# Local attention: new step orders for four engines, and new places for the first steps of the next stage

## What is computed

```python
def attn_layer(x, Wqkv, qs, ksc, Wo):            # 16 heads of 64, window 32
    q, k, v = split(x @ Wqkv)                    # 128 -> 3 x 1024
    q = l2norm(q) * qs;  k = l2norm(k) * ksc     # then a rotary embedding on both
    out = local_attention(q, k, v)               # each window sees itself and the window before it
    return out @ Wo                              # 1024 -> 128
def ffn_layer(x, g, bln, W1, b1, W2, b2):
    xn = layernorm(x) * g + bln
    a, gate = split(xn @ W1 + b1)                # 128 -> 2 x 341
    return a * gelu(gate) @ W2 + b2
for i in range(6):
    x = attn_layer(shift_tokens(x), ...) + x
    x = ffn_layer(shift_tokens(x), ...) + x
```

## Time and profile before

| what | us |
|---|---|
| median of 3 runs (lowest, highest) | 1986.94 (1985.29, 1989.4) |
| the profiled execution | 1985.58 |
| span of the profiled execution | 1983.8 |
| PE matmul busy in the span | 1823.7 |
| windowed_layers | about 109.6 to 1746 of the span |

### The profile page before, as it was taken

The page is one execution under the profiler, slowest core; times in us unless marked ns, Lnnn a source line. Parts: engine busy times, 40 slices in busy tenths (PEclk is TensorE's granted clock), DMA queues, the critical chain, the costliest instruction groups (busy, mean ns, idle before and its releaser), DMA issues. The chain is left out here.

```text
span 1983.8 us, 78949 instructions
## 1 busy us (share of the span) xinstructions
PE 1823.7 (92%) x32837; PEld 1278.3 (64%) x32837; DVE 1430.1 (72%) x2605; ACT 1138.5 (57%) x2379; POOL 1435.6 (72%) x1838
## 2 busy tenths in 40 slices
PE   4769999999999999999999999999999999788948
PEld 3636666666666666666666666666666676566638
DVE  2268778778777788787878787877788778455546
ACT  1136666666566566666666566656666666335425
POOL 1168888879788888888888788978898888222334
PEclk9789999999999999999999999999999999889969
DMA  3022131111311113111113111121111101030012
GB/s 101 1 41 56 44 99 52 47 45 51 101 48 48 51 48 100 49 50 48 48 48 103 48 48 46 34 85 32 32 35 36 42 24 35 10 98 1 23 35 71
DMA packets 60837, 99.93 MB, mean 50 GB/s; under 512 B 15848, under 2 KB 35065, under 8 KB 58643
## 3 DMA queue, kind: packets, MB, share of 16 engines
q1 hardware_dynamic: 58978, 91.72, 16.0%
q0 software_dynamic: 1504, 3.17, 0.5%
HBM read 44.50 MB, written 21.45 MB: 33 GB/s over the span
## 5 line engine op out<-in xcount | busy, mean ns | idle before, releaser
L1273 PE MATMUL b_bank_proj<-layer_weights,b_stream_t 128*128 128x512 f32 x1152 | 591.6, 615 | 13.6 <-DVE b_plain_moved L1069 9.7
L1069 DVE TENSOR_TENSOR b_plain_moved<-b_bank_proj,b_rope 128x1024 f32<-128x1024 f32 x384 | 467.6, 1221 | 100.2 <-ACT b_squares L903 96.9
L812 POOL TENSOR_TENSOR b_rotated<-b_plain_moved 128x1024 f32<-128x1024 f32 x192 | 453.4, 2361 | 45.4 <-DVE b_plain_moved L1069 45.4
L827 POOL TENSOR_TENSOR b_rotated<-b_rotated,b_inv_norm 128x1024 f32<-128x1024 f32 x192 | 365.3, 1902 | 15.1
L903 ACT ACTIVATE b_squares<-b_bank_proj 128x512 f32<-128x512 f32 x384 | 229.2, 597 | 248.4 <-PE b_bank_proj L1273 243.4
L1273 PEld LDWEIGHTS b_bank_proj<-layer_weights,b_stream_t 128*128 128x128 f32 x1152 | 187.9, 191 | 117.1 <-issue 57.1
L1075 DVE TENSOR_REDUCE b_norm<-b_squares 128x16 f32<-128x1024 f32 x192 | 232.2, 1209 | 42.7 <-ACT b_squares L903 42.4
L1281 PEld LDWEIGHTS b_bank_shared<-const_tables,b_rotated 128*128 128x128 f32 x1536 | 180.6, 143 | 72.2 <-issue 67.4
L1281 PE MATMUL b_bank_shared<-const_tables,b_rotated 128*128 128x128 f32 x1536 | 211.9, 276 | 3.8 <-POOL b_rotated L827 1.7
L832 POOL TENSOR_TENSOR b_probs<-b_probs,b_inv_sum 128x512 f32<-128x512 f32 x192 | 200.3, 1047 | 14.0 <-DVE b_inv_sum L1090 13.8
L1347 PEld LDWEIGHTS b_bank_shared<-b_attended_t,layer_weights 128*128 128x128 f32 x1536 | 182.9, 192 | 25.6 <-issue 23.9
(11 more groups left out here) (346 smaller groups left out, 2889.7 us busy)
## 6 DMA issues: line engine op xcount, KB each, us to landing
b_v_shifted<-b_v SPq DMA_DIRECT2D x192, 192.0 KB, 2.5
sorted_rows<-sorted_rows SPq DMA_DIRECT2D x66, 258.0 KB, 3.2
layer_weights<-L_ffn_Wqkv SPq DMA_DIRECT2D x6, 1536.0 KB
b_v_shifted<-b_v SPq DMA_DIRECT2D x72, 128.0 KB
layer_weights<-L_ffn_Wo SPq DMA_DIRECT2D x6, 512.0 KB
c_sorted_in<-sorted_rows SPq DMA_DIRECT2D x23, 129.0 KB, 2.0
layer_weights<-L_ffn_w SPq DMA_DIRECT2D x8, 256.0 KB, 5.9
c_w<-L_ffn_w SPq DMA_DIRECT2D x8, 256.0 KB, 5.7
```

Source lines behind the costliest of these rows:

```text
L812: nc.gpsimd.tensor_tensor(out=turned[:, k, :], in0=pm[:, k, 0, :], in1=pm[:, k, 1, :], op=ALU.add).then_inc(add_done, 1)
L827: nc.gpsimd.tensor_tensor(out=tk, in0=tk, in1=repeat_last(rn[:, k, :], DH), op=ALU.mult).then_inc(rope_done, 1)
L1069: nc.vector.tensor_tensor(to, src.to_broadcast(shape), tab.to_broadcast(shape), ALU.mult).then_inc(mul_done, 1)
L1273: nc.tensor.matmul(out, xs[:, b, t * P:(t + 1) * P], w, start=True, stop=True).then_inc(proj_full, 1)
```

## The change

All four tables are written anew, each with the steps that it had (a step may stand at another place of the turn, with another `ahead`), and the steps of the next stage hang behind other steps. No instruction is added, removed or altered; SP's list stays. The shared PSUM banks follow the new order.

```diff
--- before.py
+++ after.py
@@ -488,57 +488,58 @@
 
 
 PE_TURN = [
-    ("heads_t", 0, 0), ("heads_t", 0, 1), ("project", 0, 5), ("probs_t", -2, 1), ("project", 1, 0), ("project", 1, 1),
-    ("down", -2, 0), ("project", 1, 2), ("pv", -2, 0), ("project", 1, 3), ("heads_t", 0, 2), ("heads_t", 0, 3),
-    ("probs_t", -1, 0), ("project", 1, 4), ("scores", 0, 0), ("project", 1, 5), ("heads_t", 1, 0), ("project", 2, 0),
-    ("project", 2, 1), ("heads_t", 1, 1), ("probs_t", -1, 1), ("out", -2, 0), ("project", 2, 2), ("enter", 1, 0),
-    ("pv", -1, 0), ("project", 2, 3), ("heads_t", 1, 2), ("heads_t", 1, 3), ("out", -1, 0), ("scores", 1, 0),
-    ("back", -1, 0), ("project", 2, 4), ("project", 2, 5), ("probs_t", 0, 0), ("probs_t", 0, 1), ("heads_t", 2, 0),
-    ("project", 3, 0), ("heads_t", 2, 1), ("project", 3, 1), ("pv", 0, 0), ("project", 3, 2), ("norm_t", -1, 0),
-    ("project", 3, 3), ("out", 0, 0), ("heads_t", 2, 2), ("heads_t", 2, 3), ("up", -1, 0), ("scores", 2, 0),
-    ("up", -1, 1), ("up", -1, 2), ("up", -1, 3), ("probs_t", 1, 0), ("project", 3, 4), ("project", 3, 5),
-    ("probs_t", 1, 1), ("project", 4, 0), ("project", 4, 1), ("pv", 1, 0), ("heads_t", 3, 0), ("heads_t", 3, 1),
-    ("project", 4, 2), ("out", 1, 0), ("heads_t", 3, 2), ("heads_t", 3, 3), ("up", -1, 4), ("up", -1, 5),
-    ("leave", -2, 0), ("scores", 3, 0), ("project", 4, 3), ("project", 4, 4), ("probs_t", 2, 0),
+    ("scores", -1, 0), ("probs_t", -2, 1), ("project", 0, 5), ("project", 1, 0), ("leave", -3, 0), ("heads_t", 0, 0),
+    ("project", 1, 1), ("heads_t", 0, 1), ("down", -2, 0), ("pv", -2, 0), ("project", 1, 2), ("project", 1, 3),
+    ("heads_t", 0, 2), ("heads_t", 0, 3), ("probs_t", -1, 0), ("project", 1, 4), ("scores", 0, 0), ("heads_t", 1, 0),
+    ("project", 1, 5), ("project", 2, 0), ("probs_t", -1, 1), ("project", 2, 1), ("heads_t", 1, 1), ("out", -2, 0),
+    ("project", 2, 2), ("pv", -1, 0), ("project", 2, 3), ("heads_t", 1, 2), ("heads_t", 1, 3), ("out", -1, 0),
+    ("project", 2, 4), ("back", -1, 0), ("scores", 1, 0), ("enter", 2, 0), ("project", 2, 5), ("project", 3, 0),
+    ("probs_t", 0, 0), ("probs_t", 0, 1), ("project", 3, 1), ("heads_t", 2, 0), ("pv", 0, 0), ("project", 3, 2),
+    ("norm_t", -1, 0), ("heads_t", 2, 1), ("project", 3, 3), ("heads_t", 2, 2), ("heads_t", 2, 3), ("probs_t", 1, 0),
+    ("up", -1, 0), ("up", -1, 1), ("scores", 2, 0), ("up", -1, 2), ("up", -1, 3), ("heads_t", 3, 0),
+    ("project", 3, 4), ("project", 3, 5), ("probs_t", 1, 1), ("project", 4, 0), ("project", 4, 1), ("pv", 1, 0),
+    ("project", 4, 2), ("out", 0, 0), ("heads_t", 3, 1), ("up", -1, 4), ("up", -1, 5), ("heads_t", 3, 2),
+    ("out", 1, 0), ("project", 4, 3), ("heads_t", 3, 3), ("probs_t", 2, 0), ("project", 4, 4),
 ]
 
 
 ACT_TURN = [
-    ("heads_t", 0, 1), ("probs_t", -2, 1), ("project", 1, 2), ("root", 1, 0), ("exp", -1, 1), ("attended", -2, 0),
-    ("project", 1, 3), ("heads_t", 0, 2), ("heads_t", 0, 3), ("project", 1, 4), ("attended", -2, 1),
-    ("probs_t", -1, 0), ("project", 1, 5), ("root", 1, 1), ("project", 2, 0), ("exp", 0, 0), ("project", 2, 1),
-    ("heads_t", 1, 0), ("heads_t", 1, 1), ("probs_t", -1, 1), ("exp", 0, 1), ("root", 2, 0), ("project", 2, 2),
-    ("attended", -1, 0), ("attended", -1, 1), ("enter", 1, 0), ("project", 2, 3), ("heads_t", 1, 2),
-    ("heads_t", 1, 3), ("back", -1, 0), ("project", 2, 4), ("project", 2, 5), ("probs_t", 0, 0), ("exp", 1, 0),
-    ("probs_t", 0, 1), ("project", 3, 0), ("project", 3, 1), ("heads_t", 2, 0), ("root", 2, 1), ("heads_t", 2, 1),
-    ("attended", 0, 0), ("attended", 0, 1), ("project", 3, 2), ("project", 3, 3), ("exp", 1, 1), ("root", 3, 0),
-    ("heads_t", 2, 2), ("heads_t", 2, 3), ("gelu", -1, 0), ("gelu", -1, 1), ("gelu", -1, 2), ("probs_t", 1, 0),
-    ("project", 3, 4), ("project", 3, 5), ("probs_t", 1, 1), ("root", 3, 1), ("project", 4, 0), ("project", 4, 1),
-    ("exp", 2, 0), ("exp", 2, 1), ("attended", 1, 0), ("attended", 1, 1), ("root", 4, 0), ("project", 4, 2),
-    ("heads_t", 3, 0), ("heads_t", 3, 1), ("heads_t", 3, 2), ("heads_t", 3, 3), ("project", 4, 3), ("project", 4, 4),
-    ("exp", 3, 0), ("leave", -2, 0), ("heads_t", 4, 0), ("probs_t", 2, 0), ("project", 4, 5), ("project", 5, 0),
-    ("root", 4, 1), ("project", 5, 1),
+    ("root", -1, 1), ("heads_t", -1, 0), ("exp", -2, 0), ("project", 0, 2), ("root", 0, 0), ("exp", -2, 1),
+    ("attended", -3, 0), ("attended", -3, 1), ("heads_t", -1, 1), ("heads_t", -1, 2), ("project", 0, 3),
+    ("heads_t", -1, 3), ("project", 0, 4), ("probs_t", -2, 0), ("root", 0, 1), ("project", 0, 5), ("exp", -1, 0),
+    ("leave", -3, 0), ("project", 1, 0), ("probs_t", -2, 1), ("project", 1, 1), ("heads_t", 0, 0), ("heads_t", 0, 1),
+    ("root", 1, 0), ("exp", -1, 1), ("attended", -2, 0), ("project", 1, 2), ("project", 1, 3), ("heads_t", 0, 2),
+    ("heads_t", 0, 3), ("project", 1, 4), ("attended", -2, 1), ("root", 1, 1), ("probs_t", -1, 0), ("project", 1, 5),
+    ("project", 2, 0), ("exp", 0, 0), ("exp", 0, 1), ("project", 2, 1), ("probs_t", -1, 1), ("heads_t", 1, 0),
+    ("heads_t", 1, 1), ("project", 2, 2), ("attended", -1, 0), ("attended", -1, 1), ("root", 2, 0), ("project", 2, 3),
+    ("heads_t", 1, 2), ("heads_t", 1, 3), ("back", -1, 0), ("project", 2, 4), ("project", 2, 5), ("enter", 2, 0),
+    ("project", 3, 0), ("probs_t", 0, 0), ("probs_t", 0, 1), ("project", 3, 1), ("root", 2, 1), ("exp", 1, 0),
+    ("exp", 1, 1), ("heads_t", 2, 0), ("attended", 0, 0), ("project", 3, 2), ("attended", 0, 1), ("heads_t", 2, 1),
+    ("project", 3, 3), ("root", 3, 0), ("heads_t", 2, 2), ("heads_t", 2, 3), ("gelu", -1, 0), ("gelu", -1, 1),
+    ("probs_t", 1, 0), ("gelu", -1, 2), ("project", 3, 4), ("project", 3, 5), ("probs_t", 1, 1), ("project", 4, 0),
+    ("project", 4, 1),
 ]
 
 
 DVE_TURN = [
-    ("share", 1, 0), ("mul", 3, 2), ("scale", -1, 0), ("mul", 3, 3), ("share", 1, 1), ("norms", 3, 1),
-    ("residual", 0, 0), ("hidden", -1, 0), ("soft", 2, 0), ("soft", 2, 1), ("norms", 4, 0), ("mul", 4, 0),
-    ("share", 2, 0), ("mul", 4, 1), ("mul", 4, 2), ("share", 2, 1), ("residual", 1, 0), ("hidden", -1, 1),
-    ("hidden", -1, 2), ("soft", 3, 0), ("mul", 4, 3), ("norms", 4, 1), ("share", 3, 0), ("soft", 3, 1), ("mul", 5, 0),
-    ("norms", 5, 0), ("mul", 5, 1), ("down", -1, 0), ("mul", 5, 2), ("share", 3, 1), ("mul", 5, 3), ("norms", 5, 1),
-    ("soft", 4, 0), ("soft", 4, 1), ("mul", 6, 0), ("norms", 6, 0), ("mul", 6, 1), ("share", 4, 0),
-    ("residual", 2, 0), ("mul", 6, 2), ("share", 4, 1), ("mul", 6, 3), ("norms", 6, 1), ("residual", 3, 0),
-    ("soft", 5, 0), ("stats", 0, 0), ("soft", 5, 1), ("mul", 7, 0), ("mul", 7, 1), ("norms", 7, 0),
+    ("share", 2, 0), ("hidden", -1, 1), ("hidden", -1, 2), ("share", 2, 1), ("residual", 0, 0), ("residual", 1, 0),
+    ("mul", 4, 3), ("norms", 4, 1), ("soft", 3, 0), ("soft", 3, 1), ("share", 3, 0), ("mul", 5, 0), ("norms", 5, 0),
+    ("mul", 5, 1), ("down", -1, 0), ("share", 3, 1), ("mul", 5, 2), ("norms", 5, 1), ("mul", 5, 3), ("soft", 4, 0),
+    ("soft", 4, 1), ("mul", 6, 0), ("share", 4, 0), ("mul", 6, 1), ("norms", 6, 0), ("share", 4, 1),
+    ("residual", 2, 0), ("mul", 6, 2), ("mul", 6, 3), ("residual", 3, 0), ("norms", 6, 1), ("stats", 0, 0),
+    ("soft", 5, 0), ("soft", 5, 1), ("mul", 7, 0), ("mul", 7, 1), ("norms", 7, 0), ("share", 5, 0), ("scale", 0, 0),
+    ("mul", 7, 2), ("mul", 7, 3), ("norms", 7, 1), ("share", 5, 1), ("soft", 6, 0), ("hidden", 0, 0), ("soft", 6, 1),
+    ("mul", 8, 0), ("norms", 8, 0), ("mul", 8, 1), ("mul", 8, 2),
 ]
 
 
 POOL_TURN = [
-    ("clamp", 5, 0), ("add", 5, 0), ("rope", 5, 0), ("weigh", 3, 1), ("clamp", 5, 1), ("add", 5, 1), ("rope", 5, 1),
-    ("clamp", 6, 0), ("add", 6, 0), ("weigh", 4, 0), ("rope", 6, 0), ("weigh", 4, 1), ("add", 6, 1), ("clamp", 6, 1),
-    ("rstd", 0, 0), ("rope", 6, 1), ("clamp", 7, 0), ("add", 7, 0), ("weigh", 5, 0), ("weigh", 5, 1), ("clamp", 7, 1),
-    ("rope", 7, 0), ("add", 7, 1), ("clamp", 8, 0), ("rope", 7, 1), ("weigh", 6, 0), ("add", 8, 0), ("rope", 8, 0),
-    ("weigh", 6, 1), ("add", 8, 1), ("clamp", 8, 1), ("weigh", 7, 0), ("rope", 8, 1),
+    ("clamp", 7, 1), ("clamp", 8, 0), ("rope", 7, 1), ("add", 8, 0), ("weigh", 6, 0), ("weigh", 6, 1), ("rope", 8, 0),
+    ("clamp", 8, 1), ("add", 8, 1), ("rope", 8, 1), ("weigh", 7, 0), ("clamp", 9, 0), ("add", 9, 0), ("rope", 9, 0),
+    ("weigh", 7, 1), ("clamp", 9, 1), ("add", 9, 1), ("rope", 9, 1), ("weigh", 8, 0), ("add", 10, 0),
+    ("clamp", 10, 0), ("weigh", 8, 1), ("rope", 10, 0), ("add", 10, 1), ("clamp", 10, 1), ("rstd", 1, 0),
+    ("rope", 10, 1), ("weigh", 9, 0), ("clamp", 11, 0), ("add", 11, 0), ("rope", 11, 0), ("weigh", 9, 1),
+    ("add", 11, 1),
 ]
 
 
@@ -548,14 +549,13 @@
 
 
 FIRST = {
-    "pe": {("back", TURNS - 1, 0): ("f_weights",), ("norm_t", TURNS - 1, 0): ("f_contexts",),
-            ("up", TURNS - 1, 1): ("f_normed", "f_keys",), ("up", TURNS - 1, 3): ("f_queries",),
```

(11 more changed lines are left out.)

## The result

The changed kernel takes 2041.78 us (median of 4 runs, 2033.55 to 2054.86) against 1986.45 (4 runs, 1985.29 to 1989.4) on the same chip: a ratio of 1.028, interval 1.0253 to 1.0307. It is **slower by 55 us**, where 1981 with a range of 1965 to 1996 was forecast. Its runs also lie 21 us apart, those of before 4. The profiled execution took 2039.08 us, span 2037.3, so 53.5 us of span are to be found.

The account below looks back on a forecast made before the run. TensorE was taken to bound the kernel, 97% busy in the middle. -8.2 - 4.6 + 3.4 + 2.4 + 1.1 = -5.9 on the profiled 1985.58 gave 1979.7, as a median 1981.0 us; range 1965 to 1996.

Parts of the forecast that it names:

- Part 2: PE's dense steps: fetch waits follow the count of matmuls between them; pv gains, scores unchanged: -4.6 us, bounds -13.1 to +4.9.
- Part 5: Moves costed at nothing, such as probs_t t0.1 coming 1.30 instead of 2.60 us ahead of pv t0, called covered.
- Part 3: PE, back one projection behind out t3, ahead of scores t1: a wait of 0.14 us, 24 times, +3.4 us.
- Part 1: DVE, mul ahead of norms for the next turn's tile 0: removes 0.34 us of PE waiting a turn, -8.2 us.
- Part 4: POOL's chain behind back: heads t2.2 and probs_t t1.0 wait slightly for POOL, +2.4 us, bounds 0 and +15.8.
- Rival C: Slower: POOL becomes the bound behind back, waits of 0.66 us a turn stand; 1994 to 1997 us; chance 0.21.
- Part 6: Start and end of the stage: norms loses its free place at the start, +1.1 us; the drain 0, bounds -2 and +2.
- The rivals: Fetch waits fall by half, 1965 (0.13); nothing that can be told, 1989 or 1985.6 (0.26); slower through POOL, 1994 to 1997 (0.21).
- what would prove it wrong: L1306's waits growing over 5 us, new PE waits for POOL over 10 us in the middle, or L1335's idle time halving.
- S: The experiments' theory, not the prediction's: a late last semaphore ahead of a dense step delays the request for PE's next instruction block.

Follow-up runs that it names:

- act_probs2: Kernel before, with ACT copying the second half of t2's transposed probabilities ahead of two of its other steps, PE's order unchanged; 1976.85 us, ratio 0.9926.
- before_sc0: Kernel before, with pv of the tile two before ahead of project 1.2 on PE, instead of behind it; 2015.25 us, ratio 1.0125.
- before_back: Kernel before, with back one projection behind out t3, ahead of scores t1, and t3's residual ahead of norms on the DVE; 2006.47 us, ratio 1.0073.
- dve_mul: Kernel before, with mul ahead of norms for the next turn's tile 0 on the DVE; 1989.53 us, ratio 0.999.
- after_pv3: Changed kernel, with the old order around out t2 again on PE and ACT (project, heads, then probs_t); 2025.9 us, ratio 1.0198.
- slack_pv0: Kernel before, with act_probs2's move and the transposed shares of t0 one projection earlier on PE and ACT; 1972.48 us, ratio 0.9937.
- after_all: Changed kernel, with all six local undos together and project 1.2's square moved ahead of root, exp and copy on ACT; 2008.96 us, ratio 1.0122.

## Why the prediction was wrong, point by point

- **Part 2 failed, and with it the forecast.** Its -4.6 for the dense steps measured +39.0. The step that failed is "I count in PE_TURN the matmuls between the last pv, scores or out and each pv": act_probs2 changed the waits of pv t2 from 7.9 to 1.4 us with no matmul moved. That fetch was the cause of "issue" was right; what sets its start was not. The sentence "scores begins with eight wide mask matmuls, behind which the issue can catch up, so I leave its 15.0 as it is" failed too: 33.7. The upper bound of +9.5 for scores came from the same count (its 62 is 64 by the table) and was too low by half.
- **Part 5 failed in "It is covered".** Whether a copy is late for its step was the wrong question. A slack of 0.5 in place of 1.3 us cost pv t0 6.7 us of idle time in the stage (4.5 to 11.2). And the lead of the product over scores t0 fell from 2.55 to 1.10 us; pv ahead of project 1.2 has a share in it (1.47 in before_sc0), and no part priced that move at all.
- **Part 3** was right on back itself: PE waits at most some 0.08 us for it where 0.14 was forecast (project 2.4, ahead of it, takes 0.94 from start to start in place of 0.86). It named "scores t1" as queued behind and priced nothing for it; before_back is 14.5 us slower than before by its ratio, with 8.6 us more idle time there.
- **Part 1** was right on its pair and wrong on the sum. In the changed kernel the projection now stands straight behind pv t1:

```profile
866.04 0.83 PE L1335 MATMUL b_bank_shared<-b_probs_t,b_v 64*64 64x32 f32 x42 [1.02 <-issue]
866.80 1.13 PE L1273 MATMUL b_bank_proj<-layer_weights,b_stream_t 128*128 128x512 f32 x2
```

  The 1.21 is gone. But all steps other than pv and scores together gave +3.1 where parts 1, 3 and 4 have -2.4: heads t3.0 and t3.1 won 7.0 in the middle, and other steps (heads t2.0, project 1.4, up 1 among them) take some 0.1 us a turn more.
- **Part 4** held: PE has no idle time for POOL in the middle. Rival C's mechanism did not happen; its sign came true for another reason.
- **Part 6** looked at the wrong place: the start has +7.8 for +1.1. The first projection already starts 1.2 us later (113.3), in the stage before, which the change doesn't touch; kernels that differ as little there start it at 109.2 to 112.9. From there to the first scores, where dve_mul lost 2.5, it is 0.5. The other 6.1 stand between the first scores and out t3, where PE waits 3.6 us for POOL at heads_t and waited for none before; why POOL is late there was not tried apart. The end has +3.6 for 0, with 275.8 us; the experiments' kernels that are built on the one before and leave the end alone lie at 272.3 to 275.0, so most of it may be scatter.
- **The rivals**: none had fetch waits that double, though the text named it as what would prove it wrong. The bounds of part 2 (-13.1 to +4.9) came from one theory of the waits and its absence; a second theory of the same rows would have put the range's end elsewhere. The forecast's own upper end, 1986, was summed wrongly besides: +4.9 in place of -4.6 gives 1990.5, still far from 2041.78.

The Trainium skill ("Runtime: NRT & Kernel Launch", "Instruction fetch mechanics") has fetching run beside execution, the cost at a block's end "mostly hidden". The blocks of 256 instructions agree with the runs; "hidden" does not: pv and scores of the middle wait 33.5 us at block ends before, 66.4 after.

**What stays open.** pv t3 shows no wait at any of its 22 block ends in the kernel before, with its shares 1.23 us ahead, and none in after_pv3, with 0.20; by S it should. Its out stands close ahead; whether that is the reason was not tried. In pv t2 the distance from the copy does not hold either: 4.0 to 5.0 us before, 3.2 to 5.4 in before_sc0, and 5.1 to 6.1 in the changed kernel, where the slack is 3.00. And the spread of 21 us between the changed kernel's runs was not explained; 12 runs of dve_mul and 20 of the kernel before lie 24 and 15 us apart as well.

## What to carry to other kernels

A step of hundreds of small instructions has one more deadline than its data: the instructions themselves. Look at "issue" by step and by block end, and keep the last semaphore ahead of such a step early, those of the step before it included (here 2.65 us left pv t0 0.7 of its 4.5 us of waits, while scores t0 kept 7.7 with 2.55); a semaphore that comes just in time shows no wait of its own and still costs. When a replay or a planner counts a step as free because its data is there, check it against the step times in the trace, and judge local undos together, since each shifts the waits of the others.

## What the runs showed of the hardware that I had not expected

- In 35 waits of pv t0 and t1 (both kernels) and of scores t1 (after), TensorE went on 3.4 to 4.2 us behind the last semaphore ahead of the step, whatever the slack (0.48 to 1.30 us). With more slack it was later: 4.3 to 4.9 us in pv t0 of slack_pv0, at 2.65.
- At some of these waits the granted clock fell to the 1.2 GHz level for 3.4 or 6.8 us. The changed kernel had 8 such stretches from 215 to 1705 us, seven at a wait in pv (0.7 to 1.9 us) and one at a wait in scores (2.1 us); after_all had 2. At most of the 48 waits it did not fall.
- ACT's order alone, with no instruction of TensorE moved, took 0.7% off the kernel (act_probs2).
